# Projections in pieces between the first unit's turns, and the same groups of the loop cut in two behind the second and third head

## The reference

```python
x = x + attention(layernorm(x))     # q, k, v = n @ W + b; scores q.k/4 + slope_h*(key - 2047)
                                    # causal softmax, context @ Wo + bo
x = x + ffn(layernorm(x))           # x1 = n @ Q(w1).T, x2 = n @ Q(w2).T
                                    # (sigmoid(x1) * x2) @ Q(w3).T
# Q(w) = clip(round(w / (mean|w| + 1e-8)), -1, 1)
```

## Time and profile before

| | us |
|---|---|
| median of 3 runs | 656.02 |
| lowest, highest | 655.22, 658.75 |
| the profiled execution | 655.49 |
| its span | 653.8 |

### The profile page before, as it was taken

The page is one execution under the profiler, slowest core; times in us unless marked ns, Lnnn a source line. Parts: engine busy times, 40 slices in busy tenths (PEclk is TensorE's granted clock), DMA queues, the critical chain, the costliest instruction groups (busy, mean ns, idle before and its releaser), DMA issues.

```text
span 653.8 us, 10880 instructions
## 1 busy us (share of the span) xinstructions
PE 602.7 (92%) x3484; PEld 373.4 (57%) x3484; DVE 465.6 (71%) x1211; ACT 359.6 (55%) x766; POOL 187.3 (29%) x396
## 2 busy tenths in 40 slices
PE   7867788999899989999999999999999999999887
PEld 4544345556566646555556665555555556555486
DVE  5736688877787876677887787778788888411176
ACT  3334444755563546647655555467676665677521
POOL 7453632144432331232112331103200400424200
PEclk9978788999999989999999999999999999999989
DMA  6764644555131314534131131156141310011000
GB/s 201 247 216 110 169 112 115 138 178 145 36 99 36 81 36 111 185 100 115 35 83 34 36 99 33 51 136 147 39 111 35 83 35 1 3 44 42 1 18 33
DMA packets 27309, 57.65 MB, mean 88 GB/s; under 512 B 5044, under 2 KB 14772, under 8 KB 23796
## 3 DMA queue, kind: packets, MB, share of 16 engines
q1 hardware_dynamic: 27252, 56.95, 31.2%
HBM read 40.82 MB, written 14.80 MB: 85 GB/s over the span
## 4 chain that ended last, share of the span: by engine, by line
PE 71%; DVE 15%; issue 5%; ACT 4%; DMA 3%; SPq 1%; POOL 1%; ACTq 0%; DVEq 0%; POOLq 0%
PE pO L1069 20%; PE pS L1056 18%; PE pM L1035 16%; PE pM L1010 5%; DVE pm L1232 5%; PE pM L1019 2%; PE pM L952 2%; PE pM L996 2%; DVE pM L1235 2%; ACT probs L883 2%; DMA qst<-parts 1%; PE pS L1010 1%; DVE st L1122 1%; PE pM L960 1%; DMA parts<-qk_hl 1%
## 5 line engine op out<-in xcount | busy, mean ns | idle before, releaser
L883 ACT ACTIVATE probs<-pS 128x512 f32<-128x512 f32 (+3 forms) x640 | 301.3, 545 | 194.4 <-PE pS L1056 191.9
L1232 DVE TENSOR_REDUCE pm<-pM 128x1 f32<-128x512 f32 x384 | 238.5, 680 | 44.3 <-PE pM L1035 43.8
L1056 PE MATMUL pS<-qst,kst 128*128 128x512 f32 (+3 forms) x640 | 245.9, 404 | 6.0 <-ACT probs L883 4.2
L1035 PE MATMUL pM<-kst,qst 126*128 126x512 f32 (+3 forms) x640 | 230.7, 390 | 21.7 <-DVE pm L1235 5.4
L1056 PEld LDWEIGHTS pS<-qst,kst 128*128 128x128 f32 x640 | 120.0, 192 | 94.1 <-issue 50.3
L1035 PEld LDWEIGHTS pM<-kst,qst 126*128 126x128 f32 x640 | 122.1, 194 | 63.6 <-DVE pm L1232 15.5
L1235 DVE CUSTOM_DVE_ANT_0 pM<-pM,mask 128x128 f32<-128x128 f32 (+3 forms) x256 | 118.5, 518 | 45.1 <-PE pM L1035 44.6
L766 POOL TENSOR_SCALAR_AFFINE_SELECT probs<-probs 128x128 f32<-128x128 f32 x256 | 79.6, 323 | 240.6 <-ACT probs L883 234.0
L1069 PE MATMUL pO<-probs,vals 128*17 128x512 f32 (+3 forms) x1280 | 137.6, 545 | 0.0
L1069 PEld LDWEIGHTS pO<-probs,vals 128*17 128x17 f32 x1280 | 30.3, 98 | 68.1 <-issue 40.1
L1198 DVE SCALAR_TENSOR_TENSOR work<-work,pM 128x256 f32<-128x256 f32 (+1 forms) x38 | 15.9, 419 | 31.7 <-ACT work L873 28.1
(11 more groups left out here) (153 smaller groups left out, 409.5 us busy)
## 6 DMA issues: line engine op xcount, KB each, us to landing
kst<-parts SPq DMA_DIRECT2D x78, 256.0 KB
qst<-parts SPq DMA_DIRECT2D x30, 256.0 KB, 4.0
parts<-qk_hl SPq DMA_DIRECT2D x28, 256.0 KB, 2.9
ctx_dram<-ctx_raw SPq DMA_DIRECT2D x15, 256.0 KB, 3.8
xin<-in_L_attn_x SPq DMA_DIRECT2D x5, 512.0 KB, 5.9
out<-work SPq DMA_DIRECT2D x8, 256.0 KB, 2.2
work<-ctx_dram SPq DMA_DIRECT2D x7, 256.0 KB
work<-rden_dram SPq DMA_DIRECT2D x7, 256.0 KB
```

The source lines that it names most:

```text
L883: nc.scalar.activation(probs[:, n % PSLOTS, q0:CH], pS[:, n % SBANKS, q0:CH], ACT.Exp)\
L1035: pe.matmul(max_bank(x)[:, 0:N], qst[0:R_MAX, u % QSLOTS, h, t * P:(t + 1) * P], kst[0:R_MAX, n % KSLOTS, h, 0:N], start=True, stop=True). ...
L1056: pe.matmul(pS[:, n % SBANKS, q0:CH], kst[0:R_END, sl, h, b:b + P], qst[0:R_END, u % QSLOTS, h, q0:CH], start=True, stop=True).then_inc(sc ...
L1232: nc.vector.tensor_reduce(dst, bank, AX.X, ALU.max).then_inc(max_free, 1)
```

## The change

1. In the head, V(0,1), K(1,0) and Q(1,0) are issued in two pieces each between turns, the transposes after turns 6 and 7; Q's second piece follows the swap. K(1,1) and Q(1,1) leave the head for steps 5 and 7, chunk 1's values move to steps 1 and 2. DVE empties V(0,1) after the swap's copy. Unit 1's turns of three heads come ahead of the first scores, and the wait for empty banks stands behind them.
2. In the loop the 22 groups k, q, v and wo are cut: one piece after head 1, one after head 2, emptied after head 2.
3. The swap of a unit comes after head 0 of the step two before its first.
4. bn_stats and scaling run a row per head. x2T and the up groups behind it come a step later.
5. Down groups end with both halves of the last hidden piece; a memset moves from the last to the first split of the last half.
6. SP issues unit 2's K and Q loads ahead of K(1,0)'s store and the raw weights, and unit 3's K in step 1 instead of 3; POOL prepares slots in a matching order.

```diff
-            lst = lst[6:] + [None, ("gamma",)] + [None] * 6
+            lst = [None, lst[6], lst[7], ("gamma",), None, lst[4], None, lst[5], None, None]
...
-    TERN_STEPS, EARLY_TURNS = range(4, 10), 2
+    TERN_STEPS, EARLY_TURNS = range(4, 10), [3, 2, 2, 2, 2]
...
+    swap_in = {first_step[u] - 2: u for u in range(1, NU)}
+
+    def swap_after(s, h):
+        return swap_in.get(s) if h == 0 else None
...
-    head_between = {3 + 2 * i: g for i, g in enumerate(pre_groups(0)[-1:] + pre_groups(1)[:6])}
-    head_groups = head_first + list(head_between.values())
+    V01, XT, K10, Q10 = pre_groups(0)[-1], pre_groups(1)[:KT], ("k", 1, 0), ("q", 1, 0)
+    head_between = {3: (V01, 0), 5: (V01, 1), 6: (XT[0], None), 7: (XT[1], None), 10: (K10, 0), 12: (K10, 1), 15: (Q10, 0)}
+    head_groups = head_first + [V01, *XT, K10, Q10]
...
+    def in_pieces(g):
+
+        return g[0] in ("k", "q", "v", "wo")
+
+    def done_after(g):
+
+        return SIDE_AFTER + 1 if in_pieces(g) else SIDE_AFTER
...
-            store_parts(("k", 1, 0))
-            store_parts(("q", 1, 0))
             load_m(0)
-            store_parts(("k", 1, KT - 1))
-            store_parts(("q", 1, KT - 1))
+            load_k(2)
+            load_q(2)
+            store_parts(K10)
+            store_parts(Q10)
             load_raw(1, w2)
...
-            load_k(2)
-            load_q(2)
...
-                s = max(0, first_step[v - 1] - 5)
+                s = max(1, first_step[v - 1] - 5) if c >= 1 else 1
...
-                    for k in range(KT):
+                    for k in own:
...
+                    for f, i in [(f, i) for i in range(2) for f in range(FT - 1)] + [(FT - 1, i) for i in range(2)]:
...
             swap_max(0)
+            side_group(Q10, 1)
             pe.wait_ge(rows_ok, 1)
-            for g in head_groups:
-                if in_s_bank[number[g]] > 0:
-                    need_empty(pe, g)
...
-                early = EARLY_TURNS if j == 0 and u <= NHG else 0
+                early = EARLY_TURNS[u] if j == 0 and u <= NHG else 0
...
+                if s == 0:
+                    for g in head_groups:
+                        if in_s_bank[number[g]] > 0:
+                            need_empty(pe, g)
...
-                    if h == SIDE_AFTER and side[s]:
+                    if side[s] and in_pieces(side[s]):
+                        if h in (SIDE_AFTER, SIDE_AFTER + 1):
+                            side_group(side[s], h - SIDE_AFTER)
+                    elif side[s] and h == SIDE_AFTER:
                         side_group(side[s])
...
+                    if ph == LN_AT[c]:
+                        if h == 0:
+                            dve.wait_ge(x_in, 16 * (c + 3))
+                        ins = nc.vector.bn_stats(st[:, h, :], xin[:, h, :])
```

More of the change, by code:

```diff
@@ L196, in preln_layer @@
         ring_use += [("turn", 0, k)]
-        ring_use += ring_groups([head_between[k]] if k in head_between else [])
+        ring_use += ring_groups([head_between[k][0]] if k in head_between and not head_between[k][1] else [])
     ring_use += [("swap", 0)]
@@ L201, in preln_layer @@
             ring_use += [("turn", *use) for use in turns_after(s, h)]
-            if h == SIDE_AFTER and side[s]:
+            if side[s] and h == SIDE_AFTER:
                 ring_use += [("side", *side[s])]
-        ring_use += [("swap", step_swap[s])] if step_swap[s] else []
+            ring_use += [("swap", swap_after(s, h))] if swap_after(s, h) else []
     ring_use += ring_groups(tail_groups)
@@ L781, in _ @@
             key_rows(2)
[L782 to L788, removed]
+            query_zeros(2)
+            query_ones(2)
+            split_lo(K10)
+            split_lo(Q10)
+            key_rows(3)
             powers = 2
@@ L912, in _ @@
             size_of_weights(0)
-            for g in head_between.values():
+            for g in (*XT, K10, Q10):
                 side_op(g)
@@ L919, in _ @@
                     exps(s, h)
-                    if h == SIDE_AFTER and side[s]:
+                    if side[s] and h == done_after(side[s]):
                         side_op(side[s])
@@ L932, in _, with side_group @@
         def _(pe):
-            def side_group(g):
+            def side_group(g, piece=None):
                 kind = g[0]
-                if in_s_bank[number[g]] == 0:
+                own = range(2) if piece is None else [piece]
+                if piece == 1:
+                    pass
+                elif in_s_bank[number[g]] == 0:
                     need_ring_bank(pe, ("side", *g))
@@ L956, in side_group @@
                         pe.wait_ge(w_in, 32)
-                    for i in range(2):
+                    for i in own:
                         t = 2 * g[2] + i
@@ L1013, in side_group @@
                 elif kind == "down":
[L1014 to L1022, removed]
+                    for f, i in [(f, i) for i in range(2) for f in range(FT - 1)] + [(FT - 1, i) for i in range(2)]:
+                        if i == 0:
+                            pe.wait_ge(lo_ok, up_no[("up", g[1], g[2], f)] + 1)
+                        for part in range(2):
+                            ins = pe.matmul(w[:, i * D:(i + 1) * D], hT_of(g)[:, part, f, i * P:(i + 1) * P],
+                                            w3T[:, f, :], start=f == 0 and part == 0 and i == 0,
+                                            stop=f == FT - 1 and part == 1 and i == 1)
+                if piece != 0:
+                    ins.then_inc(side_ready, 1)
             def max_turn(u, k):
@@ L1123, in variances, with means @@
                 link(ins)
+                means(t0, t1)
+            def means(t0, t1):
                 for t in range(t0, t1):
@@ L1215, in split_hidden @@
                     need_side(dve, ("down", ups[i - 1][1], ups[i - 1][2]))
-                if m == FT - 1 and g[1:3] == (NCH - 1, 1):
-                    nc.vector.memset(hT_of(g)[rows:P, :, m, :].bitcast(F32), 0.0)
+                if m == 0 and g[1:3] == (NCH - 1, 1):
+                    nc.vector.memset(hT_of(g)[FROWS[FT - 1]:P, :, FT - 1, :].bitcast(F32), 0.0)
                 nc.vector.tensor_copy(hT_of(g)[0:rows, 0, m, :], hid[0:rows, i % 2, :]).then_inc(hi_ok, 1)
```

62 lines of the change are left out of this document (36 added, 26 removed).

## The result

| | median us | runs | ratio to before, 95% interval |
|---|---|---|---|
| before | 657.07 | 4 | |
| changed | 639.95 | 4 (638.28 to 642.20) | 0.9742 (0.9696 to 0.9789) |

The account below looks back on a forecast made before the run. PE was busy 602.7 of 653.8 us, so only idle and slow-clock time could be won. Gains summed to 21.4 us, cut by a tenth to 19; 655.49 less 19 is 636.5, plus 0.5 to the median: 637, range 628 to 649.

Parts of the forecast that it names:

- A: Head, to the first scores: they start at 36.7 instead of 42.34 us, -5.6 us, bounds -3 to -7.5.
- B: Steps 0 to 9: earlier loads, fewer waits and a faster clock, less added work, give -6 us, bounds 0 to -11.
- three swaps: Swaps that now follow their negation closely and may hold the scores behind them; priced, with stores ahead of m, at +1.3 us.
- C: Steps 10 to 17, to 124 us: norms one row per head instead of a block, -2.4 us, bounds 0 to -5.
- D: The same block of norms in the second chunk, near 234 us: -2.6 us, bounds 0 to -4.
- first x2T wait: One of two loop waits for `work`, 2.3 us in total, claimed to go as x2T moves a step later.
- E: The loop's other waits: both x2T waits and the remaining nm_hl waits go, half the latter returning; -3.2 us, bounds 0 to -5.
- F: The tail: matmuls cover the wait for the last hidden piece and a memset leaves the chain; -1.6 us, bounds -1 to -1.9.
- Rival 2: Cut groups in the loop hold a ring bank too long, about 1 us on each of 22 groups: 659 us; chance 0.05.
- Rival 1: VectorE sets steps 0 to 17, so gains of the first 124 us don't come: 10 us gained, 646; chance 0.2.
- Rival 3: The clock swings at the seams between pieces, 5% of 493 us at half speed, 12 us lost: 649; chance 0.03.
- the tenth: Cut from the summed gains of 21.4 us for waits that couldn't be named, leaving 19 us.

Follow-up runs that it names:

- a0: The changed kernel itself, unedited, timed and traced again in another group of runs: 640.37 us.
- a1: The changed kernel itself, unedited, timed and traced once more in a further group of runs: 640.41 us.
- e8: The changed kernel with V(0,1), K(1,0) and Q(1,0) whole in the head instead of in pieces: 640.27 us.
- e9: The changed kernel, but PE waits for emptied score banks ahead of unit 1's early turns, which are of two heads instead of three: 638.86 us.
- e3: The kernel before with only K(1,1) and Q(1,1) moved to steps 5 and 7 and unit 2's loads issued earlier, slots matching: 649.42 us.
- e1: The changed kernel with the swaps of units 1 to 4 back at the end of their step: 638.09 us.
- e10: The changed kernel with the swaps of units 1 to 4 at the end of their step and the loop's K and Q groups whole: 636.29 us.
- e6: The changed kernel with bn_stats, aggregation and scaling of a chunk in one block behind the step again: 644.00 us.
- e7: The changed kernel with x2T and the groups behind it a step earlier, at their old place: 644.80 us.
- e5: The changed kernel with down groups half after half again and the memset ahead of the last split: 640.32 us.
- e2: The changed kernel with the loop's 22 groups k, q, v and wo whole again, emptied after head 1: 639.08 us.
- e4: The changed kernel with raw weights issued ahead of unit 2's K and Q loads and the stores of K(1,0) and Q(1,0): 641.48 us.

## Why the prediction was right, and which terms were off

The forecast was 637 us in 628 to 649; 639.95 came. The leads below are those of the first trace, with a0 and a1 where they differ.

- **A, the head: -5.6 forecast, -7.1 measured.** Right in mechanism. The swap came at 32.09 (33.0 forecast) and waited 1.70 us for DVE, the engine that was named as the floor. e8 and e9 show that the pieces and the third head's early turns don't carry it. In e3, moving K(1,1) and Q(1,1) and the loads gave 4.2 of it. The other 3 us are DVE's: DVE begins the negation at 33.32 us in e3 and at 30.84 in the changed kernel, and one part of the negation takes 1.16 us there against 0.68. What lets it begin earlier wasn't run by itself; left by elimination are V(0,1), emptied after the swap instead of between turns, and the places of the transposes.
- **B, steps 0 to 9: -6 forecast, -1.2 measured (-2.0, -1.8).** This is the term that was mis-sized. What goes was right as far as step 4, where the lead had grown by 5.2 us. What comes was priced at 1.3 us for "three swaps"; the waits were 6.6: 1.22, 3.82 and 1.61 us, with a slow clock behind the longest. With the swaps back at their place (e1, e10) the same steps give -5.7 and -7.2, so that some 4 us of the 6.6 are lost time, and without the mispriced edit the part would have held. The price had been taken from the largest wait in before, 1.0 us. That was unit 8's swap, one head from its new place; the swaps in steps 0 to 15 moved by three heads and had not waited for theirs, so no wait of before could price them. It should have been read from what DVE has in its queue there: a ternarising op of 1.68 us and the negation, with all turns ahead of them.
- **C, steps 10 to 16: -2.4 forecast, +1.1 measured (-0.8, +0.1).** The stand behind the block fell by 1.0 us of the 1.6 forecast, and e6 shows that blocks would cost 2 to 3 us here. But the swap of unit 4 took it back (1.09 us; 1.67 in a0), and a slow clock stayed.
- **D and the first x2T wait: -2.6 and -1.1 forecast; steps 28 to 48 gave -4.6 (-4.7, -4.7).** Right, a little more. e7 takes 3.5 us of it away. e6 takes 0.5 there and 1.2 up to step 60: its 1.63 us stand is back, but not the slow stretch, which was a good part of D's price and comes and goes by itself (see the last section).
- **E: the second x2T wait gave 1.4 us from step 72 to 92** (1.2 forecast). The later swaps gave nothing: the waits on nm_hl turned into 2.2 us of waits on the ring in six, where half was expected back, and a wait for m of 0.86 us before step 32 is new.
- **F: -1.6 forecast, -1.5 where both traces have a slow stretch in the tail** (-3.0 in a0 and a1, which have none); e5 agrees by trace and can't tell by time.
- **Cutting in pieces: 0 forecast, 0 measured** (e2, e8). Rival 2, the bank held too long, exists with 1 to 2 us in all, not 22. Rival 1, gains of the first 124 us lost to VectorE, was right for about half of them: 14.0 us were forecast up to step 16, and 7.2 (9.8, 8.5) came. Rival 3 can be put aside: the clock from 110 to 604 us is 1.00.

That the total came within 3 us is in part luck. In the first trace B and C fell 8 us short of their forecasts, and a further 1.3 us of lead went in stretches that no part covers (steps 16 to 28, 48 to 72, 92 to 156). Against that stood A with 1.5 us more, D and the x2T waits with 1 more, the tenth that had been taken off the sum without a named cause (2.4), and the traces that run less at the lower clock, a0 and a1, whose spans are 17.6 and 16.4 us under before's.

Signs that were named ahead: first scores near 37 (35.24), no wait over 1 us on `qk_hl` or unit 2's rows before them (none), bn_stats of step 12 near 93 to 95 (the first at 92.81), no 1.6 us behind bn_stats (0.68 and 0.66), x2T without a wait (none). The clock over the 50 us behind the first scores was to be above 0.92, and was not: 0.87 (0.90, 0.83). The sign against, swaps of chunk 0 waiting more than 1 us each, came true four times.

## What to carry to other kernels

When a step moves closer to what produces its input, price the new wait from the producer's queue at that very place, not from the wait's largest size before; in order queues then hold everything behind it. Moves of loads and of whole groups off a chain, and one step more of distance between producer and consumer, carried this change; cutting groups in two, its name, carried nothing. And where runs of one kernel spread by 4 us, lay the same events of several traces side by side: leads of 1.4 or 4.6 us repeat to 0.1 there, as long as no slow stretch, worth some 1.5 us here, stands in one trace and not in the other.

## What the runs showed of the hardware

A tiny VectorE instruction can take seven times as long when GpSimd is at work. The negation's last part, 128x16 elements, took 0.17 to 0.28 us in before, as the row of its tile says (min, median, max in ns; the instruction ahead of it reached 1.09 us once):

```profile
L1245 DVE TENSOR_SCALAR nm_hl<-nm x16: 174/176/1087, 35.0 to 560.9; 128x16 fp32r<-128x16 f32 x16
L1246 DVE SCALAR_TENSOR_TENSOR nm_hl<-nm,nm_hl x16: 174/176/276, 35.2 to 561.1; 128x16 fp32r<-128x16 f32 x16
```

In step 6 of the changed kernel, where PE stood 3.82 us, it took 1.19. First VectorE's time line, then GpSimd's:

```profile
59.95 1.68 DVE L1360 SCALAR_TENSOR_TENSOR work<-work,thr 128x1408 bf16<-128x1408 f32 x1
61.55 0.17 DVE L1270 TENSOR_REDUCE nm<-pm 128x16 f32<-128x16 f32 x1
61.76 0.17 DVE L1271 TENSOR_SCALAR nm_hl<-nm 128x16 fp32r<-128x16 f32 x1
61.97 1.19 DVE L1272 SCALAR_TENSOR_TENSOR nm_hl<-nm,nm_hl 128x16 fp32r<-128x16 f32 x1
```

```profile
60.64 1.14 POOL L779 TENSOR_SCALAR_AFFINE_SELECT probs<-probs 128x128 f32<-128x128 f32 x1 [1.90 <-ACT probs L894]
61.87 1.26 POOL L786 TENSOR_TENSOR qk_hl<-qk_f,qk_hl 128x512 fp32r<-128x512 f32 x1
```

L1272 has two inputs in SBUF, as has K(1,1)'s low part on GpSimd, L786, which began 0.1 us earlier and ended at 63.13, just as L1272 did (63.16). The other way round, GpSimd's 128x128 select, 0.29 us elsewhere, took 1.14 us while VectorE ran its 1.68. The ten traces that have K(1,1) cut in two in the loop (the changed kernel's three, e1, and e4 to e9) all have the same pair, 1.19 to 1.20 us on VectorE beside 1.26 to 1.27. In e2 and e10, where that group is whole, the order of the two starts is reversed, by 0.02 us, and L1272 is short again; PE's wait there is 3.04 us in e2. From e10:

```profile
61.82 0.17 DVE L1272 SCALAR_TENSOR_TENSOR nm_hl<-nm,nm_hl 128x16 fp32r<-128x16 f32 x1
```

```profile
61.84 1.29 POOL L786 TENSOR_TENSOR qk_hl<-qk_f,qk_hl 128x512 fp32r<-128x512 f32 x1
```

The Trainium skill, SBUF — State Buffer, section "SBUF: two separate sides", says that VectorE and GpSimd share one pair of ports, held for a whole instruction, and names VectorE instructions with two SBUF inputs among those that need it; the traces agree, with 1 us of the 3.8 on its account. No run took one of the two away on purpose, so this rests on the order of the starts. The negation's part ahead, with one input, is held in the same way: 0.17 us as a rule, it took 1.09 us in before and 0.68 us ahead of the swap before the loop, and each time it ended 0.03 us behind a GpSimd instruction (`qk_hl`, 1.26 us) that had begun before it. Why an instruction with one input is held too, no run here shows.

The clock can make several us of difference between runs of one kernel: 0.86 or 0.93 over the same 75 us, as a0 shows above. By the mean clock of the whole span, 0.980 and 0.992, that is some 25 and 10 us at half speed, an estimate. A slow stretch isn't tied to the length of the stand ahead of it. Behind the second block of norms PE stood 1.63 us in before and fell to a slow clock; in e6 it stood 1.63 us and did not; in e1 it stood 0.66 us and did. The stretches behind these stands, of before, e6 and e1, PE's clock being the third number from the end:

```profile
234.00:237.00 3.00, 2.86 (x15) 2.50 (x19) 2.16 (x10) 0.89 (x2) 0.00 (x0) 0.55 0.01 4
227.00:231.00 4.00, 4.00 (x31) 2.27 (x30) 2.39 (x10) 1.22 (x3) 0.29 (x1) 1.00 0.00 2
219.50:223.50 4.00, 4.00 (x24) 1.88 (x23) 1.63 (x7) 0.98 (x2) 0.29 (x1) 0.67 0.00 0
```

So what an edit gains by the clock behind a stand shows in some traces only.
